# One hand-written order for fills, score pieces and products on TensorE, and maximum rows turned as a unit's second piece

## What is computed

```python
Q, K, V = heads(layernorm(x) @ Wq), heads(ctx @ Wk), heads(ctx @ Wv)
scores  = einsum('bhqd,bhkd->bhqk', Q, K) / sqrt(8)      # 256 x 1601 per head
scores  = where(mask, -inf, scores)                       # layer 3 alone
attn    = softmax(scores)                                 # minus row maximum, exp, divide by sum
x       = x + tanh(g) * (einsum('bhqk,bhkd->bhqd', attn, V) @ Wo)
x       = x + tanh(g') * feed_forward(layernorm(x))
```

## Time and profile before

| | |
|---|---|
| median of 3 runs | 1794.02 us (1792.88 to 1794.67) |
| the profiled execution's own time | 1794.01 us |
| its span, first to last instruction | 1792.3 us |
| TensorE busy | 1580.8 us (88%) |
| VectorE busy | 1338.6 us (75%) |
| ScalarE busy | 1183.6 us (66%) |
| mean granted TensorE clock | 0.912 |

### The profile page before, as it was taken

The page is one execution under the profiler, slowest core; times in us unless marked ns, Lnnn a source line. Parts: engine busy times, 40 slices in busy tenths (PEclk is TensorE's granted clock), DMA queues, the critical chain, the costliest instruction groups (busy, mean ns, idle before and its releaser), DMA issues.

```text
span 1792.3 us, 46584 instructions
## 1 busy us (share of the span) xinstructions
PE 1580.8 (88%) x15481; PEld 643.7 (36%) x15481; DVE 1338.6 (75%) x2284; ACT 1183.6 (66%) x2209; POOL 146.7 (8%) x242
## 2 busy tenths in 40 slices
PE   5599999977776999998798699999878999999967
PEld 4322222355112222223576222222353333333345
DVE  6599999556447999993686699999447777777458
ACT  3168888832442888886596388888644676667736
POOL 5000000012000000000231000000010000000012
PEclk9789999988556999999799799999986999999979
DMA  9821122106111211211021521121151111111001
GB/s 266 264 63 52 51 62 62 49 0 193 36 35 55 63 52 51 62 43 33 25 83 37 180 63 52 51 62 43 47 185 43 46 48 41 41 41 41 24 13 36
DMA packets 90147, 120.66 MB, mean 67 GB/s; under 512 B 20823, under 2 KB 62318, under 8 KB 90062
## 3 DMA queue, kind: packets, MB, share of 16 engines
q1 hardware_dynamic: 86686, 110.63, 20.9%
q0 software_dynamic: 2432, 7.94, 1.4%
q10 hardware_dynamic: 944, 0.93, 0.2%
HBM read 85.05 MB, written 34.23 MB: 67 GB/s over the span
## 4 chain that ended last, share of the span: by engine, by line
PE 60%; DVE 16%; issue 10%; DMA 6%; SPq 4%; ACT 2%; POOL 1%; DVEq 0%; ACTq 0%; POOLq 0%
PE pv_bank L1486 19%; DVE mx L1041 12%; PE exp_ring L1474 11%; PE score_ring L1444 5%; PE exp_ring L1466 4%; DMA qp<-ms 4%; PE score_ring L1448 4%; PE score_ring L1637 3%; PE exp_ring L1471 3%; PE exp_ring L1648 3%; DMA k_d<-k2c 2%; SPq L504 1%; PE score_ring L1369 1%; PE score_ring L1550 1%; PE exp_ring L1376 1%
## 5 line engine op out<-in xcount | busy, mean ns | idle before, releaser
L815 ACT ACTIVATE early<-exp_ring 128x512 f32<-128x512 f32 (+1 forms) x1728 | 933.6, 597 | 312.2 <-PE exp_ring L1474 184.4
L1041 DVE TENSOR_REDUCE mx<-score_ring 128x2 f32<-128x802 f32 (+2 forms) x832 | 758.3, 964 | 90.4 <-PE score_ring L1448 79.0
L1486 PE MATMUL pv_bank<-early,vg 128*32 128x256 f32 (+1 forms) x6912 | 567.9, 400 | 2.2 <-issue 1.5
L1448 PE MATMUL score_ring<-kp,qp 64*128 64x400 f16 (+2 forms) x1664 | 371.8, 356 | 54.1 <-DVE mx L1041 43.4
L1474 PE MATMUL exp_ring<-qp,kp 64*128 64x512 f16 (+1 forms) x1312 | 373.3, 399 | 31.1 <-DMA qp<-ms 26.0
L1486 PEld LDWEIGHTS pv_bank<-early,vg 128*32 128x32 f32 (+1 forms) x6912 | 141.5, 109 | 233.1 <-issue 129.7
L1474 PEld LDWEIGHTS exp_ring<-qp,kp 64*128 64x128 f16 (+1 forms) x1312 | 92.1, 95 | 333.4 <-ACT early L815 241.6
L1448 PEld LDWEIGHTS score_ring<-kp,qp 64*128 64x128 f16 x1664 | 85.8, 95 | 178.8 <-DVE mx L1041 153.4
L1444 PE MATMUL score_ring<-kp,qp 64*64 64x400 f16 (+1 forms) x1024 | 126.1, 352 | 11.6 <-DVE mx L1034 7.0
L1466 PE MATMUL exp_ring<-qp,kp 64*64 64x512 f16 x832 | 116.9, 398 | 0.2 <-ACT early L815 0.2
L1471 PE MATMUL exp_ring<-ctxT,mask_eye 64*64 64x512 f16 x800 | 111.5, 378 | 0.0
(11 more groups left out here) (242 smaller groups left out, 1335.1 us busy)
## 6 DMA issues: line engine op xcount, KB each, us to landing
kp<-k_d SPq DMA_DIRECT2D x128, 400.2 KB
k_d<-k1c SPq DMA_DIRECT2D x32, 400.2 KB, 6.4
qp<-q_d SPq DMA_DIRECT2D x640, 12.0 KB
ctxT<-ctxT_d SPq DMA_DIRECT2D x12, 800.5 KB, 6.2
k_d<-k2c SPq DMA_DIRECT2D x16, 400.2 KB, 6.9
k_d<-v_loc POOLq DMA_DIRECT2D x12, 400.2 KB, 9.0
ctxT_d<-ctxT SPq DMA_DIRECT2D x4, 800.5 KB, 6.0
o_all<-in_ctx SPq DMA_DIRECT2D x4, 768.0 KB
```

What stands on the lines that cost most here:

```text
L815: act.activation(pt[g][0:rows_, 2 * h:2 * h + 2, :], bank[0:rows_, :].rearrange("p (i q) -> p i q", q=S), ACT.Exp).then_inc(exped, 1)
L1041: dve.tensor_reduce(dst, src, AX.X, ALU.max).then_inc(score_free, 1)
L1448: ins = pe.matmul(pa[slot][:, z, 0:w], qp1[par][rows_, i, qt * P:qt * P + P], kp1[par][rows_, at:at + w], start=True, stop=True)
L1486: ins = pe.matmul(po[R * j:R * j + R, 0:S], vg[par][0:rows_, s, j, :], pt[g][0:rows_, j, :], start=(s == 0), stop=(s == r.kt - 1))
```

## The change

Two strings, `PLAIN` and `HIDDEN`, of 56 letters each write down one unit's order on TensorE: F is a fill, S a piece, V a product (26, 17 and 13 of them). `merged` walks the string and issues them in that order; the plain runs take `PLAIN`, the masked run `HIDDEN`, the local run keeps the formula. `turn` becomes 1 and `ahead` 9 in the four runs with a string. So a unit's 17 letters S are the last 8 pieces of unit n+1 and then 9 pieces of unit n+2, the second of which is the turn. In the last unit but one the 8 pieces come at their places and the turn takes the last S of the string. The four heads of the masked run's pieces start from the other half of the array. In VectorE's program the second unit leaves the loop and the loop's body begins one unit later; `late` is 0 in all runs, so its order of work changes only by the place of the turned rows.

```diff
--- before.py
+++ after.py
@@ -35,7 +35,6 @@
 QT = S // P
 HG = 4
 UNITS = B * H // HG
-PAUSE = 2
 PAIRS = HG // 2
 R = 32
 KQ = 3 * DH
@@ -79,6 +78,10 @@
     return banks
 
 
+PLAIN = "FVSFFVSFSFFFSVSFFVSFFVSFFSFVFSFVVSFFSFSVVSFFVSFFSVFFSVFS"
+HIDDEN = "SFVFFFSVSFFSVFSFFVSFSFVFFSFVVSFFFVSFSFSVVSFVFSFSVFSFFVSF"
+
+
 class Run:
 
 
@@ -87,9 +90,9 @@
         self.ctx = {0: 0, 2: 1, 3: 2, 4: 3}.get(index)
         self.local = nk == S
 
-        self.turn, self.ahead = (2, 5) if self.local else (3, 7)
-        self.pause = 0 if self.local else PAUSE
-        self.tail, self.gap = (3, 2) if self.local else (16, 6)
+        self.order = "" if self.local else HIDDEN if mask else PLAIN
+        self.turn, self.ahead, self.late = (2, 5, 0) if self.local else (1, 9, 0) if mask else (1, 9, 0)
+        self.tail, self.gap = 3, 2
         self.chunks = chunk_cols(nk)
         self.kt = (nk + P - 1) // P
         self.fills = PAIRS * self.kt
@@ -106,7 +109,7 @@
 
         n = len(self.chunks)
         if self.mask:
-            qt, c, i = j // (2 * HG), j // HG % 2, (0, 2, 1, 3)[j % HG]
+            qt, c, i = j // (2 * HG), j // HG % 2, (2, 0, 3, 1)[j % HG]
             return qt, [(i, 2 * c), (i, 2 * c + 1)]
         qt, c, m = j // (PAIRS * n), j // PAIRS % n, j % PAIRS
         return qt, [(m, c), (PAIRS + m, c)]
@@ -1058,19 +1061,24 @@
                     dve.tensor_copy(ms[par][:, :], pa[slot][:, 0, :].bitcast(F16)[0:HG, 0:S]
                                     ).then_inc(score_free, 1)
 
-                def unit(n, par, first=False):
-                    for k, j in r.pieces(first):
+                def unit(n, par, first=False, after_first=False):
+                    for at, (k, j) in enumerate(r.pieces(first)):
                         if j is None:
                             keep_rows(1 - par, r.slot(par, k), r.use(n, k))
                         else:
                             piece(n, par, k, j, first)
-                    keep_maxima(n, par, first)
+                        if r.late and not first and at == r.late - 1:
+                            keep_maxima(n - 1, 1 - par, after_first)
+                    if not r.late:
+                        keep_maxima(n, par, first)
 
                 unit(0, 0, first=True)
+                unit(1, 1, after_first=True)
                 with dve.Fori(0, UNITS // 2 - 1) as t:
-                    unit(2 * t + 1, 1)
                     unit(2 * t + 2, 0)
-                unit(UNITS - 1, 1)
+                    unit(2 * t + 3, 1)
+                if r.late:
+                    keep_maxima(UNITS - 1, 1, False)
                 keep_rows(1, 1, r.use0 + UNITS * r.uses - 1)
 
             def heads_out(r):
@@ -1487,13 +1495,39 @@
                                         start=(s == 0), stop=(s == r.kt - 1))
                     ins.then_inc(pv, 1)
 
+                def merged(n, par, prev, ahead, todo):
+
+                    f, p, v = 0, 0, 0
+                    for what in r.order:
+                        if what == "F":
+                            fills(n, par, f // PAIRS, f % PAIRS)
+                            f += 1
+                            if ahead is None and f == r.fills // 2:
+                                heads_out(r, range(0, NT // 2))
+                        elif what == "V":
+                            if v >= BEHIND:
+                                product(n, par, v - BEHIND)
+                            elif prev:
+                                product(n - 1, 1 - par, r.kt - BEHIND + v)
+                            v += 1
+                        else:
+                            if p < len(todo):
+                                d, k = todo[p]
+                                piece(n + d, (par + d) % 2, k, half=f % 2)
+                            elif ahead == "rest" and p == r.uses - 1:
+                                pe.wait_ge(m_ok, r.u0 + UNITS)
+                                turn(1, 1, r.use0 + UNITS * r.uses - 1)
+                            p += 1
+
                 def unit(n, par, prev=True, ahead="unit"):
 
                     todo = [(1, k) for k in range(r.ahead, r.uses)] if ahead else []
                     if ahead == "unit":
-
-                        todo += [None] * r.pause + [(2, k) for k in range(r.ahead)]
-                    elif ahead:
+                        todo += [(2, k) for k in range(r.ahead)]
+                    if r.order:
+                        merged(n, par, prev, ahead, todo)
+                        return
+                    if ahead == "rest":
                         todo += [None]
                     total, given = len(todo), 0
```

## The result

| | before | after |
|---|---|---|
| median (4 runs each) | 1794.24 us (1792.88 to 1794.67) | 1770.40 us (1766.12 to 1772.11) |
| ratio, 95% interval | | 0.9865 (0.9847 to 0.9883) |
| profiled execution, span | 1794.01, 1792.3 us | 1770.58, 1768.8 us |

A forecast was written before the change was run, and what follows sets the result against it. VectorE's reduces plus late TensorE pieces bound plain units, TensorE masked ones. Gains of 46.4 (plain), 35.8 (masked) and 6.3 (units 0 and 14), less 14.8 at run ends, make 73.7 us: 1794.02 to 1720.3 us, range 1702 to 1755.

The forecast's parts named there:

- 14.40 + .33 + .53 = 15.26: Steady plain unit on VectorE: 16 reduces of .90, .33 at the maxima, .53 for the copy; gain 1.19 per unit.
- The walk through the string: Plain unit, letter S by letter S: TensorE has .27 to 1.39 of work between pieces; no reduce later than .03.
- The local run and VectorE's re-cut loop cost nothing: the same instructions in the same order.: Local run and VectorE's loop, whose body begins one unit later: claimed cost nothing.
- 2.9 in all, of which two outstanding exponentials cover 1.0: 1.9: End of each of four runs: the first fill behind the late turn waits 2.9, costing 1.9 after cover.
- a clock of .50 past unit 0: Sign of being wrong: TensorE's clock still at the lower level after a run's first unit.
- in the walk this holds pieces back by .31, .10, .10, .31 and .10, so 18.4: Masked unit: TensorE's own 17.5 plus pieces waiting 1.15 after the reduce two before; 18.4, gain 2.75 per unit.
- The turned rows: Steady units: the rows land at 6.2, the next first fill stands at 7.5, so its wait of .55 goes.
- The first fill comes two pieces later: 2 x .90 = 1.8: Start of each of four runs: two more pieces ahead of the first fill cost 1.8.
- The exponentials' banks: Rival: fills wait for exponentials to free banks, .45 per plain and 1.2 per masked unit; 1753 us, chance .16.
- The masked order's 21.0 per unit: Rival: masked fills start strictly as written and don't overlap as balanced, 21.0 per unit; 1757 us, chance .08.
- The clock rival: Rival: TensorE's clock fails to rise in one plain run, 15 units lose 128 us; 1848 us, chance .03.
- That the order does nothing: Rival: the waits are only moved, both units stay as they are, the ends cancel; 1794 us, chance .02.

The follow-up runs named there:

- the four edits: Changed kernel with unit 14's turn back in place, VectorE's and TensorE's loops written out, first fill's input waits one fill earlier: 1724.47 us, ratio 0.9606.
- the heads' run: Changed kernel with the heads of the masked run's pieces back in the old order (0, 2, 1, 3): 1797.69 us, ratio 1.0010.
- half reduces: Kernel with the four edits, VectorE's masked reduce taken over half of its columns only (work left out): 1700.33 us, ratio 0.9476.

## Why the prediction was wrong, point by point

- **VectorE's plain unit, "14.40 + .33 + .53 = 15.26".** Right as a bound: 15.29 with the four edits. The terms shift: reduces come every .92 (13.79 from 185.40 to 199.19, for 15) rather than .90, the maxima add .11 rather than .33, the copy .52. The two errors nearly cancel, which is luck. The walk through the string was right.
- **The first step that failed: "The local run and VectorE's re-cut loop cost nothing: the same instructions in the same order."** The order of instructions was the same, but the end of the loop, behind the maxima, had lost the pause that covered it: .40 in every second unit. The same omission is in TensorE's walk: it priced letters and nothing between them. What TensorE's loop and a first fill's waits put in there cost both kinds of unit about .3. The changed plain unit is 15.70 in place of 15.26, and 39 x .44 = 17.2. The prediction priced the pause that was taken away, and not what else had stood in it.
- **The second: "the turn is the last letter S ... 2.9 in all, of which two outstanding exponentials cover 1.0: 1.9".** 2.9 was measured (2.93), but the cover was none, since ScalarE's last exponentials don't help TensorE, which has nothing to issue: 2.7 to 2.9 per run. And the clock fell behind it, for another 2.3 to 3.8 per run. Forecast 7.6, measured 23.3. The prediction named "a clock of .50 past unit 0" as a sign of being wrong, but only a failure to rise had a rival and a price.
- **The third: "in the walk this holds pieces back by .31, .10, .10, .31 and .10, so 18.4".** The gate of 1.15 was right. The slots cost 1.42 or more, and not .92, and TensorE's own order up to 17.94, and not 17.5. The loops' and waits' part, .42, comes on top: 17.94 + 1.42 + .42 = 19.78. In the place shown, a piece's wait passes to the fills and the product behind it; that this delays the next pieces' reduces in turn is argued, and not shown.
- **The turned rows.** Right: no first fill of the shown loop units waits for `qp<-ms`; it does behind the turn at the end of each run's unit 14.
- **Prologues.** "The first fill comes two pieces later: 2 x .90 = 1.8" is near in sum, +6.7 with the local run where 4 x 1.8 = 7.2 was forecast, but not part by part. Run 0's first exponential comes .1 sooner (96.73 in place of 96.83); the stretches from the last exponential before to the first of runs 2, 3 and 4 are 2.6, 1.2 and 3.4 longer. The run without the strings has the same two pieces more ahead of the fills, and over the same stretches it is .5 shorter than the kernel before. So the 1.8 isn't shown, and the sum is luck.
- **Rivals.** The exponentials' banks fall for the plain units, since the four edits reach 15.29 with the same string and the same banks; in the masked ones they may have a part in the .4 that is open, and their 1.2 per unit is not seen. The masked order's 21.0 per unit falls: with half reduces the order takes 17.94, and the heads' run shows that the halves overlap. The clock rival came in part, in unit 15, at a price of 12 us. That the order does nothing falls with the run without strings.
- **The range.** Its upper end was built on the named rivals. What was missed lies outside them all, 50 us in three parts.

## What to carry to other kernels

A walk through a new order has to price what stands between the instructions too: branches, register work and waits cost nothing while a stall covers them, and they reappear when the stall is removed. Look at what an order leaves at the ends of a run: a turn that is well covered in the loop can empty an engine in the last unit but one, and the clock can add as much again (here 11 us in units 14 and 12 in units 15). When two engines share a ring of two slots, count the waits for slots in the order too; a string that balances one engine's halves was not enough here.

## What the runs showed of the hardware

- **A loop's price.** With VectorE's loop written out, the maxima are followed by a reduce .40 sooner in the unit that had the loop's end, and 1082 instructions are gone (45502 in place of 46584), 28 branches and 1054 that work on registers. The Trainium skill (Runtime: NRT & Kernel Launch, Instruction fetch mechanics) says that a taken branch can make the sequencer wait for a fetch, and names this as one reason why kernels prefer unrolling. Both runs with a loop written out agree in their direction (ratios 0.9820 and 0.9809 against 0.9865); whether it is a fetch, no run here shows.
- **The clock after one idle.** TensorE, busy through unit 14, stood still from 331.8 to 334.5 and was then granted .58, .50 and .60 in the stretches up to 346. Products last .94 there (334.77) rather than .64. The three other runs show the same behind idle times of 2.2 to 2.7. At all four run ends the granted clock stays 1.00 when the idle time is taken away.
- **The halves.** Moving the masked pieces to the other half of the array, with nothing else changed, costs 1.72 per masked unit (21.50 in place of 19.78).
